# Moving the first layer norm's apply from ScalarE to VectorE, and each FFN phase's last residual adds from GpSimd to VectorE

## What is computed

```python
x = x + _layernorm(_L0_attn_ref(_layernorm(x), Mq, Mk, Mv))
x = x + _layernorm(_L0_ffn_ref(_layernorm(x), w_gate, w_up, w_down))
# _layernorm(x) = (x - mean) / sqrt(var + 1e-5), over the last axis
# attention: 8 heads, keys of 64, values of 128; softmax over axis 1 of (B*H, C, C)
# ffn: silu(x @ wg.T) * (x @ wu.T) @ wd.T, hidden size 3072, int32 weights / 127
```

## Time and profile before

| | us |
|---|---|
| median of the runs | 2325.81 (both runs) |
| the profiled execution | 2336.0 |
| span of its slowest core (core 3), all rows are of this core | 2334.3 |
| spans of the eight cores | 2318.5 to 2334.3 |
| mean granted TensorE clock | 0.903 to 0.906 of full speed |

### The profile page before, as it was taken

One profiled execution on the slowest core, in us unless ns is written; L12 is line 12 of the kernel. 1 busy time (PEld: TensorE's weight loads), 2 busy tenths in 40 slices (PEclk: granted clock), 3 DMA queues, 4 the chain that ended last, 5 costly groups with the idle time before them and its releaser, 6 DMA issues. The chain is left out here.

```text
span 2334.3 us, 35890 instructions; the slowest of 8 cores (2318.5 to 2334.3 us)
## 1 busy us (share of the span) xinstructions
PE 1916.5 (82%) x12864; PEld 1045.5 (45%) x12864; DVE 756.4 (32%) x1633; ACT 908.8 (39%) x1560; POOL 187.0 (8%) x150
## 2 busy tenths in 40 slices
PE   1777888888579996899952988888886999869997
PEld 1333456656335542444422435565663444334443
DVE  3112365565412212222122113655653211132211
ACT  3311688887412211311115117887873111131111
POOL 0001010010101102000020000100100000200002
PEclk9989788989689998899985998898897999979999
DMA  7069200000477503222032210000005220122201
GB/s 180 9 108 137 37 2 1 2 2 2 93 180 142 128 19 118 81 83 62 19 129 34 46 28 1 2 2 2 2 2 162 81 82 10 45 86 78 73 19 54
DMA packets 84552, 136.52 MB, mean 58 GB/s; under 512 B 29088, under 2 KB 33184, under 8 KB 84384
## 3 DMA queue, kind: packets, MB, share of 16 engines
q1 hardware_dynamic: 67744, 106.97, 14.5%
q0 software_dynamic: 16640, 27.27, 8.4%
HBM read 121.63 MB, written 35.65 MB: 67 GB/s over the span
## 5 line engine op out<-in xcount | busy, mean ns | idle before, releaser
L579 ACT ACTIVATE att<-S 128x1024 bf16<-128x1024 f32 x512 | 518.0, 1020 | 113.3 <-PE S L500 110.8
L842 PE MATMUL psG<-x2T,wgT 128*128 128x512 bf16 x1536 | 370.2, 385 | 15.2 <-ACT hT L862 15.2
L853 PE MATMUL psU<-x2T,wuT 128*128 128x512 bf16 x1536 | 364.4, 380 | 0.0
L893 PE MATMUL psD<-wdT,hT 128*128 128x512 bf16 x1536 | 332.2, 379 | 5.8 <-PEq L57 5.8
L862 ACT ACTIVATE hT<-psG 128x512 bf16<-128x512 f32 x192 | 114.5, 597 | 492.2 <-PE psG L842 492.1
L865 DVE TENSOR_TENSOR hT<-hT,psU 128x512 bf16<-128x512 bf16 x192 | 132.0, 688 | 532.6 <-PE psU L853 519.2
L461 PE MATMUL O<-v,att 128*128 128x128 bf16 x4096 | 283.2, 228 | 0.0
L461 PEld LDWEIGHTS O<-v,att 128*128 128x128 bf16 x4096 | 247.1, 102 | 48.1 <-issue 48.1
L842 PEld LDWEIGHTS psG<-x2T,wgT 128*128 128x128 bf16 x1536 | 151.0, 99 | 195.0 <-issue 23.4
L893 PEld LDWEIGHTS psD<-wdT,hT 128*128 128x128 bf16 x1536 | 150.0, 98 | 188.0 <-issue 7.7
L853 PEld LDWEIGHTS psU<-x2T,wuT 128*128 128x128 bf16 x1536 | 150.9, 98 | 183.2 <-issue 3.5
(11 more groups left out here) (82 smaller groups left out, 1064.5 us busy)
## 6 DMA issues: line engine op xcount, KB each, us to landing
wgT<-wgT_scratch SPq DMA_DIRECT2D x36, 512.0 KB, 3.8
wuT<-wuT_scratch SPq DMA_DIRECT2D x36, 512.0 KB, 4.4
x_sb<-x SPq DMA_DIRECT2D x8, 2048.0 KB, 11.6
out<-x_sb SPq DMA_DIRECT2D x32, 512.0 KB, 2.6
wdT<-wdT_scratch SPq DMA_DIRECT2D x2, 6144.0 KB, 35.1
xn_stage<-wd POOLq DMA_DIRECT2D x24, 256.0 KB, 5.6
wdT_scratch<-wks SPq DMA_DIRECT2D x24, 256.0 KB, 5.8
wgst<-wg POOLq DMA_DIRECT2D x24, 256.0 KB, 5.6
```

The costliest lines, as they stand in the source:

```text
L579: S.add("scalar", lambda sc, K=K, att_out=att_out, sl6=sl6, c=c: sc.activation(att_out, Sp[K % 2][:, :], AF.Exp, scale=0.125, accum_out=ac ...
L842: S.add("tensor", lambda tt, wsl=wsl, wcol=wcol, dt=dt, gsl=gsl, c2=c2: tt.matmul(psG[gsl][:, :], wgT_s[wsl][:, wcol + 128 * dt:wcol + 128 ...
L853: S.add("tensor", lambda tt, wsl=wsl, wcol=wcol, dt=dt, gsl=gsl, c2=c2: tt.matmul(psU[gsl][:, :], wuT_s[wsl][:, wcol + 128 * dt:wcol + 128 ...
L893: S.add("tensor", lambda tt, slot=slot, tau=tau, d2h=d2h, ht=ht, Sc=Sc: tt.matmul(psD[slot][tau][:, 512 * d2h:512 * (d2h + 1)], hT[:, 1024 ...
```

## The change

In block a1 DVE applies the norm in place of ACT, as `(x + (-mean)) * rstd`; `nmr1` is now `-mean`, made in one small DVE instruction in place of two. ACT keeps Ln, Exp and the copies. In block b2 the two adds of the last chunk (Sc = 3) are made by DVE, with a semaphore of their own; the stores of that chunk wait for the six adds of the other chunks on POOL and for their own add. Chunks 0 to 2 stay on POOL.

```diff
+    s_xadd3d = S.sem("s_xadd3d")
...
-            nm1_done = S.add("vector", lambda v, g4=g4, mean_v4=mean_v4: v.tensor_tensor(
-                nmr1[:, 4 * g4:4 * g4 + 4], mean_v4, rstd1[:, 4 * g4:4 * g4 + 4], AL.mult),
+            negm_done = S.add("vector", lambda v, g4=g4, mean_v4=mean_v4: v.tensor_scalar(
+                nmr1[:, 4 * g4:4 * g4 + 4], mean_v4, -1.0, None, AL.mult),
                 waits=[(c_act, rstd_done)], inc=c_dve)
-            negm_done = S.add("vector", lambda v, g4=g4: v.tensor_scalar(
-                nmr1[:, 4 * g4:4 * g4 + 4], nmr1[:, 4 * g4:4 * g4 + 4], -1.0, None, AL.mult),
-                waits=[(c_dve, nm1_done)], inc=c_dve)
             for t in tiles:
-                S.add("scalar", lambda sc, t=t: sc.activation(
+                S.add("vector", lambda v, t=t: v.tensor_scalar(
                     xn_bf[:, D * (t % 2):D * (t % 2 + 1)], x_sb[:, D * t:D * (t + 1)],
-                    AF.Identity, bias=nmr1[:, t:t + 1], scale=rstd1[:, t:t + 1]),
+                    nmr1[:, t:t + 1], rstd1[:, t:t + 1], AL.add, AL.mult),
                     waits=[(c_dve, negm_done), (s_tp, tp_base + t - 1)], inc=s_xn)
...
+            add_d = {}
...
+                    if Sc == 3:
+                        add_d[tau] = S.add("vector", lambda v, slot=slot, tau=tau, tt_idx=tt_idx: v.tensor_tensor(
+                            x_sb[:, D * tt_idx:D * (tt_idx + 1)],
+                            x_sb[:, D * tt_idx:D * (tt_idx + 1)],
+                            u2[:, 2048 * slot + 1024 * tau:2048 * slot + 1024 * (tau + 1)],
+                            AL.add),
+                            waits=[(s_ap3, ap3_base + 2 * Sc + tau + 1)], inc=s_xadd3d)
+                    else:
+                        S.add("gpsimd", ...)   # as before
...
+                    stw = ([(s_xadd3, xadd3_base + 6), (s_xadd3d, add_d[tau])]
+                           if Sc == 3 else
+                           [(s_xadd3, xadd3_base + 2 * Sc + tau + 1)])
```

More of the change, by code:

```diff
@@ L936, in build @@
                     tt_idx = 8 * H + 2 * Sc + tau
[L937 to L942, removed]
+                    if Sc == 3:
[6 more added lines that the diff above has]
+                    else:
+                        S.add("gpsimd", lambda p, slot=slot, tau=tau, tt_idx=tt_idx: p.tensor_tensor(
+                            x_sb[:, D * tt_idx:D * (tt_idx + 1)],
+                            x_sb[:, D * tt_idx:D * (tt_idx + 1)],
+                            u2[:, 2048 * slot + 1024 * tau:2048 * slot + 1024 * (tau + 1)],
+                            AL.add),
+                            waits=[(s_ap3, ap3_base + 2 * Sc + tau + 1)], inc=s_xadd3)
                 for tau in range(2):
                     tt_idx = 8 * H + 2 * Sc + tau
+                    stw = ([(s_xadd3, xadd3_base + 6), (s_xadd3d, add_d[tau])]
+                           if Sc == 3 else
+                           [(s_xadd3, xadd3_base + 2 * Sc + tau + 1)])
                     S.add("sync", lambda s, tt_idx=tt_idx, b=b: s.dma_start(
@@ L947, in build @@
                         x_sb[:, D * tt_idx:D * (tt_idx + 1)]),
-                        waits=[(s_xadd3, xadd3_base + 2 * Sc + tau + 1)],
+                        waits=stw,
                         inc=q_st[tt_idx // 4], amt=16)
```

## The result

| | before | changed |
|---|---|---|
| median of the runs, us | 2326.96 (8 runs) | 2272.49 (9 runs) |
| ratio, with its 95% interval | | 0.9765 (0.9754 to 0.9776) |
| spans of the eight cores in the profiled execution, us | 2318.5 to 2334.3 | 2261.0 to 2270.1 |
| mean granted TensorE clock | 0.903 to 0.906 | 0.903 to 0.912 |

The change takes 54.5 us off, 2.35%. The forecast was 54.4 us and 2271.4 us. With any of the kernels some executions run longer, with a lower granted clock on half of the cores; the ratios leave these out.

A forecast was written before the change was run, and what follows sets the result against it. The prediction took block a1's chain through ACT's queue and POOL's last adds at four block ends to bound the kernel. Savings of 45.2 + 9.2 = 54.4 us took 2325.8 to 2271.4 us, range 2262 to 2283.

The forecast's parts named there:

- What bounds the stage: Block a1: apply, transposes and copy form a chain through ACT's queue, 15.21 us per four tiles, with no engine full.
- The sum of part 1: Block a1, norm's apply moved to DVE: 22.57 us less in batch 0, 22.62 in batch 1, 45.2 in sum.
- apply on VectorE: Block a1: one apply from SBUF on DVE was taken at 0.75 us, with 1.34 kept for the range.
- first to second pair of transposes: Block a1: tile 0's transposes at a + 0.89, tile 2's at a + 3.15, a being the group's first apply.
- period of a group: Block a1: four tiles, with statistics now unhidden on DVE, take 10.39 us in place of 15.21.
- L558's rate: Rival, block a1: each apply takes 1.34 us, as the same operation does from PSUM; 44.5 us saved, 2281.3 us; chance 0.14.
- The clock case: Rival, projection start: unpaused transposes bring TensorE's clock up earlier, 1.9 us a batch less, 2267.6 us; chance 0.12.
- The data: Batch 0's start: last load lands at about 44 us, before group 3's statistics at 46.8, so it stays hidden.
- Part 2: Four down projection block ends: last two adds on DVE, about 1.2 us each, take 2.3 us off each, 9.2 in all.
- The slower side: Rival, block a1: each apply waits behind a pair of POOL instructions, 39.8 us more per batch, 2396 us; chance 0.02.
- The total: Whole kernel: 45.2 us from block a1 plus 9.2 from the block ends, 54.4 us off, to 2271.4 us.

The follow-up runs named there:

- the applies shared: Against the changed kernel, block a1's applies were split per group: tiles 0 and 1 on VectorE, 2 and 3 on ScalarE; ratio to before 0.9787.
- GpSimd's adds: The changed kernel with 19 extra 128x1024 adds on GpSimd at the start of each block a1; ratio to before 0.9908.

## Why the prediction was right

**What bounds the stage.** Right. The forecast held that the stage is a chain through ACT's queue and that no engine is full; with the apply gone from that queue the chain was shorter by the amount worked out.

**The sum of part 1.** From the first transposes to the last ones the forecast went from 56.4 us (80.22 - 23.85, rows 4 and 5) to 35.45 - 0.89 = 34.6, 21.8 less. Measured from the first transposes to the first projection matmul, over eight cores, it went from 57.24 to 35.47, 21.8 less. Term by term there are small differences that cancel:

| term | forecast | measured |
|---|---|---|
| apply on VectorE | 0.75 | 0.812 |
| apply to apply, back to back | 0.66 | 0.73 |
| small instruction to the apply behind it | 0.27 | 0.35 |
| first to second pair of transposes | 2.26 | 2.26 |
| period of a group | 10.39 | 10.46 |
| start of the stage in each batch | 0.8 earlier | 0.7 earlier |

The second pair's start is a right number for a wrong reason, and so luck: I had PE's own length as the limit, at 2.14 us for two tiles. The two tiles take 1.86, and the trace names ACT's copy of the tile two before (`s_evT`), with 0.4 us of waiting.

**L558's rate.** The fork that decided between 2.3% and 1.9% went to the row that I had taken, from SBUF. The argument by bytes read was sound for the choice, but it is no law: the form without per-partition scalars reads the same 4 KB and takes 0.693, L521 0.753 with one scalar. The experiment with the doubled apply shows what the other branch would have been: an apply step of 1.45 us costs about 8 us a batch.

**The clock case.** I had given it 0.12 as a rival of its own, up to 1.9 us a batch. It came true in part, beside the forecast's case. From the first projection matmul to the mv issue it is 30.05 and 30.04 us in the two batches before and 28.8 and 28.9 in the changed kernel, 1.3 and 1.1 less, with the same matmuls. It is with the pauses that this goes: with the doubled apply, which puts 0.43 us between the transposes of one tile and the next, it is 29.3 and 29.9; with the applies shared, 30.1 in both; with GpSimd's adds, which leave the last two groups as they are in the changed kernel, 28.7 in both. The granted clock at the start of batch 1's projection, first of before, then of the changed kernel:

```profile
1283.00:1285.00 2.00, 2.00 (x10) 0.90 (x9) 0.00 (x0) 1.01 (x1) 0.00 (x0) 0.50 0.00 0
1285.00:1287.00 2.00, 2.00 (x6) 0.76 (x5) 0.00 (x0) 0.00 (x0) 0.00 (x0) 0.50 0.00 0
1287.00:1288.00 1.00, 1.00 (x6) 0.44 (x5) 0.69 (x1) 0.00 (x0) 0.00 (x0) 0.98 0.00 0
```

```profile
1224.50:1226.00 1.50, 1.50 (x6) 0.59 (x5) 0.00 (x0) 1.31 (x2) 0.00 (x0) 0.50 0.00 0
1226.00:1228.00 2.00, 2.00 (x9) 0.83 (x8) 0.48 (x1) 0.00 (x0) 0.00 (x0) 0.86 0.00 0
```

In before it is at the low level for nearly 4 us behind 1283.3; in the changed kernel for some 2 us behind 1224.5. In batch 0 the profile has no record of the clock ahead of its first change and prints 1.00, but the matmuls show the same. Two stretches of before, behind the first projection matmul at 81.0 us:

```profile
83.00:85.00 2.00, 2.00 (x6) 0.74 (x5) 0.25 (x1) 0.00 (x0) 0.00 (x0) 1.00 0.00 0
85.00:87.00 2.00, 2.00 (x10) 0.82 (x9) 0.44 (x1) 0.03 (x1) 0.00 (x0) 1.00 0.00 0
```

The first ones start 0.43 us apart and the later ones 0.22. Counted over the eight cores, 8.0 and 7.9 such slow steps open the projection in the two batches before, 1.9 and 2.4 in the changed kernel (0 to 5 on single cores). At 0.21 us each this is 1.3 and 1.2 us, the whole difference. So the term that the forecast had left at nothing measured 1.2 us a batch. This is what makes the a1 stages 23.7 and 23.5 in place of 22.6.

**The data.** The forecast had batch 0's last load landing at about 44 us and the statistics of group 3 at 46.8. The changed kernel starts them at 46.64 with no wait. The row for the second half of that argument, TensorE's and the DMA engines' stretch from 43 to 48 us in before (DMA share 0.17, 31 GB/s), is this one; the earlier trace rows hold only the landing times:

```profile
43.00:48.00 5.00, 1.48 (x13) 0.97 (x10) 0.00 (x0) 3.09 (x4) 0.00 (x0) 1.00 0.17 31
```

The forecast had left open whether the loads of mq and mk, issued by GpSimd, suffer from applies on VectorE. Over the eight cores they take 27.6 and 41.7 us to land in batch 0 before and 27.6 and 42.1 in the changed kernel, and in batch 1 14.8 and 19.8 before and 15.1 and 19.9 in the changed kernel. They do not, where both are issued ahead of the first apply.

**Part 2.** The add was put at 1.2 us and takes 1.222; both adds were to end 3.65 after ACT's start and end 3.67 after it. At three of four ends the next block starts 2.1 to 2.3 us earlier. The step that was mis-sized is the fourth, the end of the kernel: 1.7, not 2.3. The two stores now start 1.1 us apart, where it was 2.3. Over the eight cores the last one takes 2.8 us to land in place of 2.6, and the last instruction of all comes 0.7 us behind the landing in place of 0.3; these two make up the 0.6. Why the landing is seen later is open.

**The slower side.** Not reached, and the runs say how near it was. Beside GpSimd's adds the applies start 2.3 us apart; the break-even of the whole change was put at 2.66. The adds beside two of the four groups made the way from the first transposes to the projection 11.1 and 12.2 us longer. By an estimate from this, adds beside all four would cost some 22 to 24 us a batch, as much as the move of the apply had brought there (21.8).

**The total.** That 54.4 met 54.5 to 0.1 us is luck. The parts were off by 2.0 us in the a1 stages (47.2 in place of 45.2, mostly the clock) and by 0.9 the other way at the block ends (8.3 in place of 9.2), and the medians of the kernel before differ by up to 3.7 us from chip to chip.

## What to carry to other kernels

An engine that is 60% busy in a stage can still bound it, if its in-order queue holds two links of the same chain; moving one link to an engine with slack can shorten the chain by more than the link's own length (here 21.8 us over 16 tiles, 1.36 a tile, with a link of 1.24, although the statistics became serial), and the new period could be summed from rows of the old trace to within 0.1 us. Ask in the same breath what the receiving engine did there until now (here statistics) and who shares its memory access. Then look where the idle time has gathered: here the larger follow-up gain lay in work for TensorE that could be put into the pauses left, not in speeding up the chain once more.

## What the runs showed of the hardware that I had not expected

- Transposes did not reliably hold TensorE's clock: at the upper level after 12 matmuls of 512 columns, it fell to 1.2 GHz within the four tiles' transposes that followed (0.69, then 0.50 granted) on five of eight cores, and stayed up on three. Yet transposes without pause ahead of the projection went with a low-clock start of the projection that was 1.2 us shorter.
- With the q matmuls between the transposes the clock is still low in three of the four groups of batch 0 (chunks of 9.98, 8.75 and 8.75 us, and one of 7.07), so part of what filling the pauses should have brought went to the clock.
- VectorE's tensor_scalars of 4 elements per partition can be held up by GpSimd's adds as well, up to 1.33 us in place of 0.17, while bn_stats of 512 elements beside the same adds stay at 0.68.
- The first per-partition scalar of a 128x1024 tensor_scalar costs 0.05 us, the second, with its add, 0.07.
- At the start of the kernel the profile prints a granted clock of 1.00 while matmuls of 512 columns start 0.43 us apart, twice the 0.22 of later ones.
